# Causal mask on VectorE instead of TensorE, and a new order of the work around softmax, in a one-core transformer layer

## What is computed

```python
x = x + attn(dynamic_conv(x, cond))       # 1x1 convolution over the 32 channels with weights per sequence,
                                          # then causal attention over the 32 tokens, 32 query heads of 16,
                                          # 8 key/value heads, rotary positions
x = x + ffn(grouped_conv(x, cond))        # grouped convolution of 9 taps along the 512 features,
                                          # then x @ W.T + b and a LoRA of 8 experts of rank 16,
                                          # weighed by a softmax router over 15 outputs
# inside attn:
scores = jnp.einsum('bkgqd,bkmd->bkgqm', qg, k) / np.sqrt(HEAD_DIM)
scores = jnp.where(causal, scores, -jnp.inf)
attn = jax.nn.softmax(scores, axis=-1)
out = jnp.einsum('bkgqm,bkmd->bkgqd', attn, v)
```

## Time and profile before

| | us |
|---|---|
| timed runs, median of 3 | 666.9 (661.57 to 669.52) |
| profiled execution, its own time | 660.26 |
| profiled execution, first to last instruction (span) | 658.5 |
| TensorE busy in the span | 615.5 |
| VectorE busy | 476.7 |
| GpSimd busy | 225.4 |
| ScalarE busy | 194.8 |

### The profile page before, as it was taken

One profiled execution on the slowest core, in us unless ns is written; L12 is line 12 of the kernel. 1 busy time (PEld: TensorE's weight loads), 2 busy tenths in 40 slices (PEclk: granted clock), 3 DMA queues, 4 the chain that ended last, 5 costly groups with the idle time before them and its releaser, 6 DMA issues.

```text
span 658.5 us, 12838 instructions
## 1 busy us (share of the span) xinstructions
PE 615.5 (93%) x4347; PEld 512.3 (78%) x4347; DVE 476.7 (72%) x1168; ACT 194.8 (30%) x443; POOL 225.4 (34%) x182
## 2 busy tenths in 40 slices
PE   5898999999999999999999999999999999999775
PEld 3577888878888888788888887888888878888554
DVE  3357787777787777777877777778777777787743
ACT  4233323323232233232322332323223323233210
POOL 7434233333332333333323333333233333333310
PEclk9869999999999999999999999999999999999998
DMA  7575453533445543334455433344555333444430
GB/s 177 116 232 139 104 120 89 118 79 82 117 116 120 120 111 95 78 82 116 116 120 120 117 93 83 75 115 117 118 120 119 96 84 76 108 118 101 105 80 33
DMA packets 121300, 71.20 MB, mean 108 GB/s; under 512 B 48341, under 2 KB 103285, under 8 KB 121032
## 3 DMA queue, kind: packets, MB, share of 16 engines
...
q10 hardware_dynamic: 864, 0.14, 0.1%
...
## 4 chain that ended last, share of the span: by engine, by line
PE 78%; DVE 7%; issue 6%; ACT 3%; DMA 3%; DVEq 1%; SPq 1%; POOL 0%; ACTq 0%
PE ps L392 33%; PE ps L556 9%; PE ps L550 8%; PE ps L608 5%; PE ps L568 5%; PE ps L576 5%; PE ps L523 4%; DVE qk_t L1043 3%; ACT raw L686 3%; PE ps L596 2%; PE ps L564 2%; DMA scratch<-x_dram 2%; PE ps L524 1%; PE ps L487 1%; DMA x_dram<-x1p 1%
## 5 line engine op out<-in xcount | busy, mean ns | idle before, releaser
L858 POOL TENSOR_TENSOR qk<-network,t 128x640 f32<-128x640 f32 x32 | 49.8, 1557 | 181.9 <-DVE t L1035 181.9
L392 PE MATMUL ps<-wqkv_hi,y_hi 128*128 128x512 f32 (+1 forms) x256 | 87.8, 343 | 0.3 <-DVE raw L1054 0.3
L392 PE MATMUL ps<-wqkv_hi,y_lo 128*128 128x512 f32 (+1 forms) x256 | 87.3, 341 | 0.0
L392 PE MATMUL ps<-wqkv_lo,y_hi 128*128 128x512 f32 (+1 forms) x256 | 87.2, 341 | 0.0
L1149 DVE TENSOR_TENSOR x1p<-ps,xr 128x512 f32<-128x512 f32 x32 | 35.3, 1102 | 60.9 <-PE ps L392 60.9
L870 POOL TENSOR_TENSOR raw<-x1p,basebB 128x512 f32<-128x512 f32 x32 | 48.8, 1526 | 65.1 <-DVE x1p L1149 65.1
L686 ACT ACTIVATE qk_t<-ps 128x512 f32<-128x512 f32 x32 | 19.1, 597 | 140.3 <-PE ps L541 140.3
L840 POOL TENSOR_TENSOR raw<-raw,rz 128x512 f32<-128x512 f32 x32 | 33.7, 1052 | 75.8 <-DVE rz L1064 75.8
L742 ACT ACTIVATE raw<-raw 128x512 f32<-128x512 f32 x64 | 40.5, 632 | 63.4 <-DVE raw L1054 63.4
L1052 DVE TENSOR_REDUCE mx<-ps 128x16 f32<-128x512 f32 x64 | 43.9, 686 | 17.8 <-PE ps L568 17.8
L686 ACT ACTIVATE raw<-ps 128x512 f32<-128x512 f32 x64 | 34.8, 595 | 71.8 <-PE ps L596 71.8
...
## 6 DMA issues: line engine op xcount, KB each, us to landing
...
vB<-v_dram SPq DMA_DIRECT2D x128, 16.0 KB, 2.1
...
```

The source lines that it names most:

```text
L392: last = mm(dst, a, b, start=(n == 0), stop=(n == 3 * len(left) - 1))
L858: nc.gpsimd.tensor_tensor(qk[:, :], t1, t2[:, :], ALU.add).then_inc(qk_sb, 1)
```

## The change

- **Mask.** `scores` starts its banks with the products of q and k alone. `softmax` first adds the mask from the constants to the scores, PSUM into `sx`, and takes the maximum and the subtraction in place on `sx`. The banks are free for the next q, k and v from the addition on (`sm0_sb` instead of `sx_sb`).
- **k first.** `transpose_qk` transposes k ahead of q, with a semaphore of its own, and `keys` waits for it. x1 of the pass before, which was the last of VectorE's pass, is now behind `keys` in the next.
- **P in three parts.** The eight transposed tiles of P are handed over and copied as two, four and two (banks 2, 3 and 5).
- **values ahead of hw.** `values` comes before `transpose_hw`.
- **Start.** `prepare_conv` and `prepare_ar` move behind the first k and v products (pass -1); `prepare_conv` uses bank 3. Pass 0 has the order of the other passes. VectorE adds qk of group 0 instead of GpSimd. The mixing weights of groups 1 to 3 go by ScalarE's queue, and SyncE's waits for them come later. GpSimd's `first_half` is always behind y_lo.
- **End.** In pass 32 `lora` comes before the convolution, with 28 products (`keep_warm`) between them, whose result nobody reads, and VectorE does the output sum before the convolution's bias.

```diff
+        def load_mixw(eng, lo, hi, done):
+
+            for b in range(NB):
+                eng.dma_start(mixw[S * b:S * (b + 1), lo:hi, b, :],
+                              mixw_dram.rearrange("(g b) i o -> b i g o", b=NB)[b, :, lo:hi, :]).then_inc(done, 16)
...
             mixb_row = mixb_dram.rearrange("b s -> (b s)")
             sp.wait_ge(y_ps, 1)
             sp.dma_start(xm[:, :], group(x_g, 1)).then_inc(xm_in, 16)
-            sp.wait_ge(mixw_zero, 1)
-            sp.wait_ge(aggw_act, 1)
-            sp.wait_ge(aggw_dve, 1)
-            sp.dma_start(mixw_dram[NB:4 * NB, :, :], aggS[NB:4 * NB, :, :]).then_inc(mixw_out1, 16)
             sp.wait_ge(aggb_dram, 16)
             sp.dma_start(mixb[:, P:4 * P], mixb_row[P:4 * P].partition_broadcast(P)).then_inc(mixb_in, 16)
-            sp.wait_ge(mixw_out1, 16)
-            load_mixw(1, 4, mixw_in2)
...
             load_values(0)
             sp.dma_start(xr[:, :], group(x_g, 0)).then_inc(xr_in, 16)
             sp.dma_start(rawbase, baseW.rearrange("(p j) l -> p j l", j=PH)).then_inc(ld["base"], 16)
+            sp.wait_ge(mixw_zero, 1)
+            sp.wait_ge(aggw_act, 1)
+            sp.wait_ge(aggw_dve, 1)
             sp.dma_start(mixw_dram[4 * NB:B, :, :], aggS[4 * NB:B, :, :]).then_inc(mixw_out, 16)
             sp.wait_ge(mixw_out, 16)
-            load_mixw(4, G, mixw_in)
+            load_mixw(sp, 4, G, mixw_in)
             sp.dma_start(mixb[:, 4 * P:], mixb_row[4 * P:].partition_broadcast(P)).then_inc(mixb_in2, 16)
...
+            def keep_warm(products):
+
+                for _ in range(products):
+                    mm(ps[:, 0, :], query16[0:S, :], causal16[0:S, :], start=True, stop=True)
...
                 if live(u - 1):
-                    pe.wait_ge(sx_sb, 2 * (u - 1) + 1)
+                    pe.wait_ge(sm0_sb, 2 * (u - 1) + 1)
...
+                nc.tensor.transpose(ps[:, 5, 0:P], qk[:, D:D + P], ident).then_inc(kT_ps, 1)
                 for g in range(NQ):
-                    nc.tensor.transpose(ps[:, 4, g * P:(g + 1) * P], qk[:, g * P:(g + 1) * P], ident)
-                nc.tensor.transpose(ps[:, 5, 0:P], qk[:, D:D + P], ident).then_inc(qT_ps, 1)
+                    last = nc.tensor.transpose(ps[:, 4, g * P:(g + 1) * P], qk[:, g * P:(g + 1) * P], ident)
+                last.then_inc(qT_ps, 1)
...
-                for h in range(2):
-                    rows = slice(h * P // 2, h * P // 2 + S)
-                    mm(ps[:, h, :], query16[rows, :], causal16[rows, :], start=True, stop=False)
                 for b in range(NB):
                     for h in range(2):
                         rows = slice(h * P // 2, (h + 1) * P // 2)
                         last = mm(ps[:, h, b * P:(b + 1) * P], qT[rows, b, :, :].rearrange("p g q -> p (g q)"),
-                                  kT[rows, b, :, :].rearrange("p k m -> p (k m)"), start=False, stop=(b == NB - 1))
+                                  kT[rows, b, :, :].rearrange("p k m -> p (k m)"), start=True, stop=True)
...
-                        last = nc.tensor.transpose(ps[:, 2 + n // 4, (n % 4) * P:(n % 4 + 1) * P],
+                        bank, at = ((2, n), (3, n - 2), (3, n - 2), (5, n - 6))[b]
+                        last = nc.tensor.transpose(ps[:, bank, at * P:(at + 1) * P],
                                                    pr[:, (NB * h + b) * P:(NB * h + b + 1) * P], ident)
-                    if b % 2:
+                    if b != 1:
                         last.then_inc(pT_ps, 1)
 
             def values(t):
 
                 pe.wait_ge(vB_in, 16 * HK * (t + 1))
                 for b in range(NB):
-                    if b % 2 == 0:
-                        pe.wait_ge(pT_sb, 2 * t + 1 + b // 2)
+                    if b != 2:
+                        pe.wait_ge(pT_sb, 3 * t + (1, 2, 2, 3)[b])
...
-                if live(t + 1) and not peeled(t, 0):
+                if peeled(t, 0):
+                    pe.wait_ge(mixw_in2, 16 * NB)
+                if live(t + 1):
                     mix(t + 1)
                 if peeled(t, -1):
                     mixing_weights()
@@ -635,14 +638,6 @@
                 if live(t):
                     scores(t)
 
-                if peeled(t, 0):
-                    prepare_ar()
-                    prepare_conv()
-                    pe.wait_ge(mixw_in2, 16 * NB)
-                    mix(t + 1)
-                    transpose_p(t)
-                    pe.wait_ge(convW_sb, 1)
-                    values(t)
                 if peeled(t, 1):
                     pe.wait_ge(prep_sb, 1)
                     prepare_base((0, 1))
@@ -652,18 +647,26 @@
                     queries(t + 1)
                     keys_values(t + 1)
 
-                if live(t) and not peeled(t, 0):
+                if peeled(t, -1):
+                    prepare_conv()
+                    prepare_ar()
+                if peeled(t, 0):
+                    pe.wait_ge(convW_sb, 1)
+                if live(t):
                     transpose_p(t)
+                if live(t):
+                    values(t)
                 if live(t - 2):
                     transpose_hw(t - 2)
-                if live(t) and not peeled(t, 0):
-                    values(t)
+                if peeled(t, G):
+                    lora(t - 2)
+                    keep_warm(28)
                 if live(t - 1):
                     conv(t - 1)
                 if peeled(t, 1):
                     prepare_base((2, 3))
 
-                if live(t - 2):
+                if live(t - 2) and not peeled(t, G):
...
+                act.wait_ge(aggw_act, 1)
+                act.wait_ge(aggw_dve, 1)
+                act.dma_start(mixw_dram[NB:4 * NB, :, :], aggS[NB:4 * NB, :, :]).then_inc(mixw_out1, 16)
+                act.wait_ge(mixw_zero, 1)
+                act.wait_ge(mixw_out1, 16)
+                load_mixw(act, 1, 4, mixw_in2)
...
-                    for h in range(2):
-                        act.wait_ge(pT_ps, 2 * t + 1 + h)
-                        copy(prT[:, 4 * h:4 * h + 4, :].rearrange("p k n -> p (k n)"), ps[:, 2 + h, :]).then_inc(pT_sb, 1)
+                    for n, (bank, lo, hi) in enumerate(((2, 0, 2), (3, 2, 6), (5, 6, 8))):
+                        act.wait_ge(pT_ps, 3 * t + 1 + n)
+                        copy(prT[:, lo:hi, :].rearrange("p k n -> p (k n)"), ps[:, bank, 0:(hi - lo) * P]).then_inc(pT_sb, 1)
...
-                if live(t) and peeled(t, 0):
-                    first_half(t)
                 if live(t + 1) and not peeled(t, -1):
                     pool.wait_ge(y_hi_sb, t + 2)
                     nc.gpsimd.tensor_tensor(y_lo[:, :], ys[:, :], y_hi[:, :].bitcast(F32),
                                             ALU.subtract).then_inc(y_lo_sb, 1)
+                if live(t):
+                    first_half(t)
                 if peeled(t, 0):
                     prepare_wo((2, 3))
-                elif live(t):
-                    first_half(t)
-                if live(t + 1):
+                if live(t + 1) and not peeled(t, -1):
...
-                dve.wait_ge(qT_ps, t + 1)
+                dve.wait_ge(kT_ps, t + 1)
...
-                    v.tensor_reduce(m, s3, AX.X, ALU.max).then_inc(mx_sb, 1)
+                    sx3 = sx[:, D * h:D * h + D].rearrange("p (h m) -> p h m", m=S)
+                    v.tensor_tensor(sx3, s3, cst[:, C_CAUSAL:C_CAUSAL + S].unsqueeze(1).broadcast_to([P, 16, S]),
+                                    ALU.add).then_inc(sm0_sb, 1)
+                    dve.wait_ge(sm0_sb, 2 * t + 1 + h)
+                    v.tensor_reduce(m, sx3, AX.X, ALU.max).then_inc(mx_sb, 1)
                     dve.wait_ge(mx_sb, 2 * t + 1 + h)
-                    v.tensor_tensor(sx[:, D * h:D * h + D].rearrange("p (h m) -> p h m", m=S), s3,
-                                    m.unsqueeze(2).broadcast_to([P, 16, S]), ALU.subtract).then_inc(sx_sb, 1)
+                    v.tensor_tensor(sx3, sx3, m.unsqueeze(2).broadcast_to([P, 16, S]), ALU.subtract).then_inc(sx_sb, 1)
...
             def steps(t):
                 if live(t):
                     keys(t)
+                if live(t - 1):
+                    dve.wait_ge(wo_ps, t)
+                    dve.wait_ge(xr_in, 16 * t)
+
+                    wait(dve, x1c_sb, t - 1)
+                    wait(dve, x1_out, 16 * (t - 1))
+                    v.tensor_tensor(x1, ps[:, 3, :].rearrange("p (j n) -> p j n", j=PH),
+                                    xr[:, :].rearrange("p (n j) -> p j n", j=PH), ALU.add).then_inc(x1_sb, 1)
                 if live(t - 2):
                     dve.wait_ge(z_hi_sb, t - 1)
                     minus(z_lo[:, :, :].rearrange("p j (q o) -> p j q o", o=CG), z_transposed(),
@@ -1092,7 +1125,9 @@
                     dve.wait_ge(mixb0_sb, 1)
                 if peeled(t, 3):
                     dve.wait_ge(mixb_in2, 16)
-                if live(t + 1) and not peeled(t, 0):
+                if peeled(t, 0):
+                    dve.wait_ge(mixb_in, 16)
```

(39 more changed lines are left out.)

34 lines of the change are left out of this document (20 added, 14 removed).

## The result

| | before | after |
|---|---|---|
| timed, median (4 runs each, side by side) | 667.0 us (661.57 to 669.52) | 674.07 us (672.6 to 675.01) |
| ratio, with its 95% interval | | 1.0128 [1.0081, 1.0174] |
| profiled execution, span | 660.3 us, 658.5 us | 672.6 us, 670.8 us |

What follows compares the result with a forecast made beforehand. TensorE was taken to bound the loop, with VectorE close behind. Start -4, loop -9.5, pass 31 -1 and end +4.6 made -9.9 us on the profiled 660.3, or 656 us by ratio on the timed median; range 646 to 666.

Steps and rivals of the forecast that it cites:

- the chain that decides: Loop: VectorE's last product at 9.22, low_oT at 14.80; the projection waits 0.18 us, a pass takes 18.44 us.
- Pass 0's gain: Start: prepare_ar and prepare_conv, 4.4 us at clock 0.50, go off the path of pass 0.
- Pass 2 at +1: Start: VectorE already decides pass 2, so the two masks come in full, less what reordering hides: +1 us.
- the first half's subtraction: Loop, VectorE: beside GpSimd's y_lo the subtraction takes 811 ns instead of 693, adding 0.12 us; the second half's does not.
- A product of that width: End, pass 32: each of the 28 products of 512 columns takes 0.23 us, 6.4 us together; the end is +4.6.
- the bound (+11): End, pass 32: the upper bound on the +4.6 us, if the 28 products run at half clock.
- (c): Rival: the 28 products run at half clock or the start gains nothing; 6 us less gain, near 662; chance 0.15.
- the start's sum: Start: work moved off TensorE's path, waits removed and added, clock regained earlier; -5 us, with pass 2's +1 making -4.
- P in three copies: Loop, TensorE: copies of two, four and two tiles take 2.54 us against 2.40, a cost of 0.14.
- (b): Rival: VectorE becomes the bound, 0.12 more on six instructions, a pass of 19.0, 674 us; chance 0.09.
- (a): Rival: in the loop TensorE never waits for VectorE; 18.12 to 18.26 a pass, about 650 us; chance 0.22.
- (d): Rival, end: the 28 products hide behind the transfer because the convolution's data comes later than now; 652 us; chance 0.06.

Runs made afterwards that it cites:

- hw_first: The changed kernel with hw transposed ahead of `values` again: 690.99 us, period 19.267.
- ylo_late: The changed kernel with GpSimd's y_lo made to wait for VectorE's first subtraction on sx: 668.63 us, period 18.467.
- mask_alone: The kernel before with only the mask moved to VectorE, all else unchanged: 684.2 us, period 19.403.
- mixb_later: The changed kernel with xm's load issued ahead of mixw_dram's store and mixb's load cut in two, the rest behind xc's loads of pass 2: 668.56 us.
- pe_split_now: The changed kernel without the 28 products, mask on TensorE, hw ahead of `values`, P in two copies, mixb's load cut in two: 649.40 us, ratio 0.9772.
- p_two_ylo: ylo_late with P copied in two parts of four tiles, as before the change: period 18.564 against 18.467.
- mask_pe: The changed kernel with the mask back on TensorE as two causal products, no addition on VectorE: 665.44 us, period 18.633.

## Why the prediction was wrong

**Right.** `scores` directly behind `mix` at 1.97, P's transposition at 10.96 (11.02), the convolution 2.54 behind (2.57). The swap of hw and `values` as what makes the mask affordable (hw_first: 0.57 a pass without it). VectorE's last product and low_oT as the chain that decides, with little between the engines (forecast at 9.22 and 14.80, measured at 9.59 and 14.99; ylo_late shortens the chain and the pass). Pass 0's gain: first transposition of pass 1 at -4 (forecast -5). Pass 2 at +1: it lasts 20.04 (70.22 to 90.26) against 19.09 (68.98 to 88.07). And that the 28 products do not hide behind the convolution's transfer.

**Wrong, first: "the first half's subtraction (4.6 to 5.4) runs beside GpSimd's y_lo, the second does not: +0.12".** The mechanism was right and the size was off by a factor of four: +0.49. I took 811 ns in L1068 as the price of lying beside GpSimd. But L1068 at 302.57 lies beside GpSimd's L840 only until 302.83, for 0.26 of its 0.69 us. The row for it in the kernel before:

```profile
301.78 1.05 POOL L840 TENSOR_TENSOR raw<-raw,rz 128x512 f32<-128x512 f32 x1 [2.13 <-DVE rz L1064]
```

y_lo covers nearly all of the subtraction, and the price goes by the overlap: L1064 reads two operands from SBUF and loses most of the time that both run.

| row | both run, us | above 0.69, us |
|---|---|---|
| L1068 in the kernel before | 0.26 | 0.12 |
| mask_alone, first half | 0.47 | 0.33 |
| after, first half | 0.63 | 0.49 |
| hw_first, first half | 0.65 | 0.51 |
| ylo_late; after, second half | 0 | 0 |

The rows of mask_alone, in VectorE's and GpSimd's timelines: 

```profile
328.51 1.02 DVE L1055 TENSOR_TENSOR raw<-raw,mx 128x512 f32<-128x512 f32 x1
...
327.69 1.29 POOL L847 TENSOR_TENSOR y_lo<-ys,y_hi 128x512 fp32r<-128x512 f32 x1 [0.93 <-ACT y_hi L683]
```

From 0.26 to 0.63 us of overlap the loss grows from 0.12 to 0.49: it is the overlap less about 0.14. The Trainium skill (GPSIMD Engine Reference, Specifications) names the contention of two SBUF inputs, and the trace agrees in which of the two halves pays. That section gives no size; the sizes here are those of the table. The 0.37 that I was short went through the chain: VectorE's product 0.37 late, low_oT 0.19, the projection 0.23 (15.82 after the start of the pass, forecast 15.59), the pass 18.70 for 18.44. Times 28 that is 7 us, the loop's whole shortfall. With the price taken away (ylo_late) the pass is 18.467, the forecast within 0.03.

**Wrong, second: "A product of that width takes 2.85/12 = 0.24 in the projection, I take 0.23: 6.4 us".** They took 12.05 us, 0.43 each. The price was that of products over 128 rows at full clock. TensorE had idled 1.50, 1.14 and 0.78 us in pass 32 up to lora, the granted clock fell to 0.50 in the last of lora's products, and it did not come back under products over 32 rows. I named half clock as the bound (+11) and as rival (c), and put it at 6 us; the end came to +13.2, beyond the bound, because what follows ran at half clock as well: the convolution 1.93 where I had counted 1.07 (before it took 1.75, so it was at half clock there, too), and granted clock 0.60 from there to the end, where the kernel before, behind its convolution, had 0.89. Up to z's transposition the loss is 11.4 us, behind it 1.8. In the windows view, after and then before:

```profile
641.00:653.50 12.50, 12.50 (x34) 4.12 (x36) 1.06 (x2) 0.00 (x0) 1.04 (x1) 0.50 0.06 22
653.50:670.80 17.30, 10.59 (x43) 8.08 (x35) 4.84 (x16) 1.56 (x5) 0.00 (x0) 0.60 0.04 16
```

```profile
645.50:658.50 13.00, 5.98 (x37) 5.09 (x35) 5.22 (x17) 1.57 (x5) 1.04 (x1) 0.89 0.11 42
```

**Wrong, third: the start's sum, "-4.4 - 0.7 - 0.9 + 1.2 + 1.5 - 1.7".** Every term in it is work of TensorE or its waiting for another engine; none is for a transfer of SP's. Work was taken off TensorE's path, and next in line was a transfer whose issue is tied to mixw_dram's store, not to TensorE, and which lands behind 1792 KB. The row for it, 7.1 us to landing at worst, was in the trace of before and leaves 0.8 us. So the -4 at the start of pass 1 was +1.2 at its end, with the half clock behind the wait as part of it, and pass 2's +1 came on top, with small waits (0.31 for hw, 0.23 for hwT_lo); `scores` directly behind `mix` gives 0.4 back, which makes the +1.8. mixb_later and pe_split_now show the gain where the transfers allow it.

**Wrong, fourth and small:** P in three copies was to cost 0.14. It gains 0.10 in this order (p_two_ylo). The measured 2.57 stands close to my 2.54; it was the alternative that I had wrong.

**The rivals.** (c) was the nearest, and happened in both of its parts at once, though I had it stop at 662. (b), slower with VectorE as the bound, had the right engine and the right instruction at the end of the chain, but the price on one instruction, not on six, and the pass stayed below the 18.78 of before. That its 674 us are the measured 674.07 is chance: it had +7 in the loop, which measured -2.3. (a) and (d) fell. What all of them missed is that three terms could fail at once.

**Open.** Why the loss from GpSimd is the overlap less some 0.14 us, and whether that holds for GpSimd instructions of other forms, was not tried. Nor was what lets the clock fall at the end of lora in the changed kernel and later in others: in mask_pe some of the 28 products still ran at full clock (10.04 us for all), in the changed kernel none did. And `lora` ahead of the last convolution was never tried apart from the rest of the change.
